# Query, key and value projections in three rounded passes, for two sequences at once

## The reference, cut to what matters

```python
# 1. retention: 16 heads of 16, over the 32 sequences
qkv = x @ W_qkv;  q, k, v = split(qkv)
ret = einsum('bhtd,bhsd->bhts', q, k) * decay          # causal decay mask
r = einsum('bhts,bhsd->bhtd', ret, v) + (q @ past_kv) * 256
x = layernorm(x + groupnorm(r))
# 2. causal attention of x over ctx (keys and values from ctx)
q = x @ Wq.T;  k = ctx @ Wk.T;  v = ctx @ Wv.T
x = layernorm(x + softmax(causal(q k^T / 4)) @ v @ Wo.T + bo)
# 3. two of 8 experts for each token, hidden size 1024
x = layernorm(x + sum over the top two of gate_e * (gelu(x @ w_fc[e] + b_fc[e]) @ w_proj[e] + b_proj[e]))
```

## Time and profile before

| | us |
|---|---|
| median of 3 runs | 1039.97 (1038.79 to 1041.47) |
| the profiled execution, its own time | 1039.19 |
| its span | 1037.0 |
| PE busy | 961.4 (93%) |
| DVE busy | 657.6 (63%) |
| ACT busy | 590.1 (57%) |

### The profile page before, as it was taken

The page is one execution under the profiler, slowest core; times in us unless marked ns, Lnnn a source line. Parts: engine busy times, 40 slices in busy tenths (PEclk is TensorE's granted clock), DMA queues, the critical chain, the costliest instruction groups (busy, mean ns, idle before and its releaser), DMA issues.

```text
span 1037.0 us, 30058 instructions
## 1 busy us (share of the span) xinstructions
PE 961.4 (93%) x10909; PEld 846.7 (82%) x10909; DVE 657.6 (63%) x2020; ACT 590.1 (57%) x1533; POOL 372.3 (36%) x630
## 2 busy tenths in 40 slices
PE   6799999999999999999988898999999999999950
PEld 4688888888888888888867897999999999999950
DVE  2456767667677677777764565665575765575537
ACT  3355555555555555555555564665575665575534
POOL 0224544445444444444453432322223222223223
PEclk9799999999999999999998999999999999999985
DMA  8101151111111111113011234442525342522327
GB/s 271 52 23 53 38 181 42 54 63 38 58 43 53 63 38 59 42 54 108 23 48 42 47 73 122 103 81 41 142 42 133 92 92 41 141 43 42 48 39 317
DMA packets 56931, 79.91 MB, mean 77 GB/s; under 512 B 5681, under 2 KB 45873, under 8 KB 56561
## 3 DMA queue, kind: packets, MB, share of 16 engines
q1 hardware_dynamic: 41072, 58.50, 17.3%
q0 software_dynamic: 13536, 18.16, 10.1%
q10 hardware_dynamic: 2208, 1.73, 0.6%
HBM read 52.10 MB, written 29.71 MB: 79 GB/s over the span
## 4 chain that ended last, share of the span: by engine, by line
PE 65%; DVE 16%; ACT 5%; issue 5%; POOL 4%; DMA 3%; SPq 1%; ACTq 0%; DVEq 0%; POOLq 0%
PE bank L724 15%; PE bank L738 10%; DVE row_max L1111 7%; PE bank L483 5%; PE bank L740 5%; PE bank L598 3%; PE bank L498 3%; PE bank L473 3%; PE bank L551 3%; PE bank L643 3%; PE bank L523 3%; PE bank L629 2%; ACT h_f L1017 2%; PE bank L518 2%; POOL grstd L1487 2%
## 5 line engine op out<-in xcount | busy, mean ns | idle before, releaser
L724 PE MATMUL bank<-xs_hi,w_both 128*128 128x256 f32 x1152 | 242.2, 287 | 0.1
L1011 ACT ACTIVATE h_hi<-bank,bfc_s 128x256 fp32r<-128x256 f32 x288 | 139.6, 485 | 163.0 <-PE bank L724 157.5
L1529 POOL DMA_INDIRECT residual_sum<-y_w,meta_i x72 | 116.6, 1619 | 308.1 <-DVE y_w L1356 284.2
L1314 DVE TENSOR_TENSOR h_lo<-h_f,h_hi 128x256 fp32r<-128x256 f32 x288 | 121.6, 425 | 150.6 <-ACT h_f L1017 146.5
L738 PE MATMUL bank<-w_both,h_hi 128*128 128x512 f32 x544 | 200.5, 398 | 1.3 <-DVE h_lo L1314 1.2
L724 PEld LDWEIGHTS bank<-xs_hi,w_both 128*128 128x128 f32 x1152 | 191.5, 190 | 8.4 <-issue 2.2
L724 PE MATMUL bank<-xs_lo,w_both 128*128 128x256 f32 x576 | 162.9, 283 | 0.0
L740 PE MATMUL bank<-w_both,h_lo 128*128 128x256 f32 x544 | 153.2, 282 | 0.0
L1017 ACT ACTIVATE h_f<-bank,bfc_s 128x256 f32<-128x256 f32 x288 | 138.9, 482 | 4.3 <-DVE h_lo L1314 3.6
L738 PEld LDWEIGHTS bank<-w_both,h_hi 128*128 128x128 f32 x544 | 102.8, 189 | 20.2 <-DVE h_lo L1314 3.7
L724 PEld LDWEIGHTS bank<-xs_lo,w_both 128*128 128x128 f32 x576 | 109.8, 191 | 0.1
(11 more groups left out here) (167 smaller groups left out, 1928.9 us busy)
## 6 DMA issues: line engine op xcount, KB each, us to landing
rows<-sent_rows SPq DMA_DIRECT2D x37, 258.0 KB
xcT<-in_turned SPq DMA_DIRECT2D x32, 256.0 KB, 2.7
w_raw<-in_w_fc SPq DMA_DIRECT2D x8, 1024.0 KB
w_raw<-in_w_proj SPq DMA_DIRECT2D x8, 1024.0 KB
x_t<-in_x SPq DMA_DIRECT2D x32, 128.0 KB, 2.6
residual_sum<-x_row SPq DMA_DIRECT2D x32, 128.0 KB, 1.7
last_in<-residual_sum SPq DMA_DIRECT2D x8, 512.0 KB, 7.3
result<-last_out SPq DMA_DIRECT2D x8, 512.0 KB, 2.6
```

Of the source, the lines that this page charges most:

```text
L724: last = mm(ps_h(g, j), w[:, at:at + P], v[:, k, :], start=(n == 0), stop=(n == 3 * NCH - 1))
L1011: A(h_hi[j % 4][:, :], ps_h(g, j), ACT.Gelu_apprx_tanh, bias=bias)
L1314: V.tensor_tensor(h_lo[j % 4][:, :], h_f[j % 2][:, :], h_hi[j % 4][:, :].bitcast(f32), ALU.subtract).then_inc(s["h_split"], 1)
L1529: G.indirect_dma_start(total, bass.IndirectOffsetOnAxis(meta_i[:, half:half + 1], 0), y_w[:, half, :], None, compute_op=ALU.add)\
```

## The change

The projections no longer use float32 matmuls. Each operand is split into a rounded part (`_hi`, made by an ACT copy) and the rest (`_lo`, a DVE subtraction), and three matmuls of rounded operands, hi by hi, hi by lo and lo by hi, take the place of one. The queries and keys are computed for two sequences at once (`pair_run`, m = 0 to 15), 256 columns in each matmul: `prep_k(m)` and `prep_q(m)` stand in the odd steps, `prep_kx(m)` in the even ones, `prep_v` in each step for the next sequence. Each of the four is 12 matmuls of 256 columns, recorded at L500. Activations are loaded for a pair at once (`load_turned`), split by `x_high` on ACT and `x_low` on DVE, one half in each step. In even steps `att_scores` moves ahead of `att_proj` and `qx`. The weights are split once before the first step (`w_high`, `w_low`). The output biases of experts 1 to 7 (`bproj_rest`) are loaded after the steps, into space that the attention has left. The stages that are kept stand in the order that they had on DVE, ACT and POOL; on ACT the copies of the projections follow their stages.

The core of the diff:

```diff
-        h_hi = [sb(f"h_hi{i}", [P, SLOT], f32r) for i in range(4)]
-        h_lo = [sb(f"h_lo{i}", [P, SLOT], f32r) for i in range(4)]
+        h_parts = sb("h_parts", [P, 8, SLOT], f32r)
+        h_hi = [h_parts[:, i, :] for i in range(4)]
+        h_lo = [h_parts[:, 4 + i, :] for i in range(4)]
+        xc_hi = [h_parts[:, 4 * i:4 * i + 4, :].rearrange("p (a k) n -> p a k n", a=2) for i in range(2)]
...
+        def over(name, shape):
+            with ExitStack() as raw:
+                loaded = raw.enter_context(nc.sbuf_tensor(name + "_raw", shape, f32))
+            return loaded, ab(name + "_lo", shape, f32r)
+        wqk_raw, wqk_lo = over("wqk", [P, NCH, 2 * C])
...
+        xc_raw, xc_lo = zip(*(over(f"xc{i}", [P, 2, NCH, 2 * T]) for i in range(2)))
+        qkT = ab("qkT", [P, 2, NCH, 2 * T])
+        q_own = ab("q_own", [P, NCH, PAIR, 2 * T])
+        kxT = [ab(f"kxT{i}", [P, NCH, 2 * T]) for i in range(2)]
...
+            def load_turned(m, a):
+                if m >= 2:
+                    sp.wait_ge(s["prep_v"], 2 * m - 2)
+                    apart(sp)
+                sp.dma_start(xc_raw[m % 2][:, a, :, :].rearrange("p k t -> p (k t)"),
+                             turned[m, :, a * 2 * C:(a + 1) * 2 * C]).then_inc(s_turned[m % 2][a], 16)
...
+            load_turned(0, 0)
+            sp.dma_start(wqk_raw[:, :, :], w_qkv[:, 0:2 * C].rearrange("(k p) n -> p k n", p=P))\
+                .then_inc(s["got_wqk"], 16)
+            load_turned(0, 1)
...
+                if k >= 0 and k % 2:
+                    for a in range(2):
+                        pair_run(load_turned, (k + 3) // 2, a)
...
+            sp.dma_start(bproj_rest[:, :, :].rearrange("p e c -> p (e c)"),
+                         b_proj[1:E, :].rearrange("e c -> (e c)").partition_broadcast(P)).then_inc(s["got_bias"], 16)
...
-            def prep_qk(c):
-                pe.wait_ge(s["kx_out"], c.n + 1)
+            def three(to, passes):
+                last = None
+                for n, (left, right) in enumerate(passes):
+                    last = mm(to, left, right, start=(n == 0), stop=(n == len(passes) - 1))
+                return last
+            def channels(m, a, w_hi, w_lo, first_col):
+                x_hi, x_lo = xc_hi[m % 2], xc_lo[m % 2]
+                for j in range(NCH):
+                    at = slice(first_col + j * P, first_col + (j + 1) * P)
+                    last = three(ps_prep[:, j * 2 * T:(j + 1) * 2 * T],
+                                 [(w[:, k, at], v[:, a, k, :]) for k in range(NCH)
+                                  for w, v in ((w_hi, x_hi), (w_hi, x_lo), (w_lo, x_hi))])
+                return last
+            def prep_k(m):
+                if m:
+                    pe.wait_ge(s["v_out"], 2 * m)
+                else:
+                    pe.wait_ge(s["w_split"], 1)
+                pe.wait_ge(s["xc_split"], 2 * m + 1)
+                channels(m, 0, wqk_hi, wqk_lo, C).then_inc(s["prep_k"], 1)
+            def prep_q(m):
+                pe.wait_ge(s["k_out"], m + 1)
+                if m == 0:
+                    pe.wait_ge(s["w_split"], 2)
+                channels(m, 0, wqk_hi, wqk_lo, 0).then_inc(s["prep_q"], 1)
+            def prep_kx(m):
+                pe.wait_ge(s["v_out"], 2 * m + 1)
+                if m == 0:
+                    pe.wait_ge(s["w_split"], 4)
+                channels(m, 1, wk_hi, wk_lo, 0).then_inc(s["prep_kx"], 1)
+            def prep_v(c):
+                m, h = c.n // 2, c.n % 2
+                if h:
+                    pe.wait_ge(s["kx_out"], m + 1)
+                else:
+                    pe.wait_ge(s["q_out"], m + 1)
+                    pe.wait_ge(s["xc_split"], 2 * m + 2)
                 if first(c, 1):
-                    pe.wait_ge(s["got_wqk"], 16)
-                for m in range(2 * NCH):
-                    for k in range(NCH):
-                        last = mm(ps_prep[:, m * P:(m + 1) * P], wqk_s[:, k, m * P:(m + 1) * P],
-                                  xcT[c.r][:, 0, k, :], start=(k == 0), stop=(k == NCH - 1))
-                last.then_inc(s["prep_qk"], 1)
-            def prep_kx(c):
-                pe.wait_ge(s_turned[c.r], 16 * (c.g + 1))
-                if not first(c, 1):
-                    pe.wait_ge(s["v_out"], c.n)
-                if first(c, 1):
-                    pe.wait_ge(s["got_wk"], 16)
-                for m in range(NCH):
-                    for k in range(NCH):
-                        last = mm(ps_prep[:, m * P:(m + 1) * P], wk_s[:, k, m * P:(m + 1) * P],
-                                  xcT[c.r][:, 1, k, :], start=(k == 0), stop=(k == NCH - 1))
-                last.then_inc(s["prep_kx"], 1)
-            def prep_v(c):
-                pe.wait_ge(s["qk_out"], c.n + 1)
-                if first(c, 1):
-                    pe.wait_ge(s["got_wv"], 32)
-                for i, w in enumerate((wvr_s, wva_s)):
-                    for k in range(NCH):
-                        last = mm(ps_prep[:, i * C:(i + 1) * C], xcT[c.r][:, i, k, :], w[:, k, :],
-                                  start=(k == 0), stop=(k == NCH - 1))
+                    pe.wait_ge(s["w_split"], 3)
+                at = slice(h * T, (h + 1) * T)
+                x_hi, x_lo = xc_hi[m % 2], xc_lo[m % 2]
+                for a in range(2):
+                    last = three(ps_prep[:, a * C:(a + 1) * C],
+                                 [(v[:, a, k, at], w[:, a, k, :]) for k in range(NCH)
+                                  for v, w in ((x_hi, wv_hi), (x_hi, wv_lo), (x_lo, wv_hi))])
                 last.then_inc(s["prep_v"], 1)
...
             def step(k):
+                odd = k % 2
                 run(ret_scores, At(k))
                 run(att_back, At(k - 3))
                 run(x1_turn, At(k - 1))
-                run(prep_v, At(k))
+                if odd:
+                    pair_run(prep_k, (k + 1) // 2)
+                else:
+                    run(att_scores, At(k - 2))
                 run(att_proj, At(k - 3))
                 run(qx, At(k - 1))
-                run(att_scores, At(k - 2))
+                if odd:
+                    run(att_scores, At(k - 2))
                 run(ret_values, At(k))
                 run(rank, At(k - 4))
-                run(prep_kx, At(k + 1))
+                if odd:
+                    pair_run(prep_q, (k + 1) // 2)
+                else:
+                    pair_run(prep_kx, k // 2)
                 run(x2_turn, At(k - 3))
                 run(gn_mean, At(k))
                 run(y_back, At(k))
                 run(max_scores, At(k - 1))
                 run(att_values, At(k - 2))
-                run(prep_qk, At(k + 1))
+                run(prep_v, At(k + 1))
                 run(logits, At(k - 3))
...
+            def x_high(m, a):
+                act.wait_ge(s_turned[m % 2][a], 16 * (m // 2 + 1))
+                A(xc_hi[m % 2][:, a, :, :], xc_raw[m % 2][:, a, :, :], ACT.Copy)\
+                    .then_inc(s["xc_high"], 1)
+            def k_out(m):
+                act.wait_ge(s["prep_k"], m + 1)
+                A(qkT[:, 1, :, :].rearrange("p k t -> p (k t)"), ps_prep[:, :], ACT.Copy).then_inc(s["k_out"], 1)
+            def q_out(m):
+                act.wait_ge(s["prep_q"], m + 1)
+                A(qkT[:, 0, :, :].rearrange("p k t -> p (k t)"), ps_prep[:, :], ACT.Copy)
                 for j in range(PAIR):
-                    last = A(q_own[:, :, j, :], ps_prep[:, 0:C].rearrange("p (k t) -> p k t", k=NCH), ACT.Copy,
+                    last = A(q_own[:, :, j, :], ps_prep[:, :].rearrange("p (k t) -> p k t", k=NCH), ACT.Copy,
                              scale=own_head[j])
-                last.then_inc(s["qk_out"], 1)
-            def kx_out(c):
-                act.wait_ge(s["prep_kx"], c.n + 1)
-                A(kxT[c.r][:, :, :].rearrange("p k t -> p (k t)"), ps_prep[:, 0:C], ACT.Copy)\
+                last.then_inc(s["q_out"], 1)
+            def kx_out(m):
+                act.wait_ge(s["prep_kx"], m + 1)
+                A(kxT[m % 2][:, :, :].rearrange("p k t -> p (k t)"), ps_prep[:, :], ACT.Copy)\
                     .then_inc(s["kx_out"], 1)
...
+                if k == -1:
+                    act.wait_ge(s["got_small"], 16)
+                    w_high(0)
+                    x_high(0, 0)
+                    w_high(1)
+                    x_high(0, 1)
+                    w_high(2)
                 run(att_back_out, At(k - 3))
                 run(x1_T_out, At(k - 1))
-                run(v_out, At(k))
+                if k >= 0:
+                    pair_run(x_high, (k + 2) // 2, odd)
+                if odd:
+                    pair_run(k_out, (k + 1) // 2)
                 run(qx_out, At(k - 1))
                 for r in range(2):
                     run(att_exp, At(k - 2), r)
                 run(y_out, At(k))
                 for r in range(2, NT):
                     run(att_exp, At(k - 2), r)
-                run(kx_out, At(k + 1))
                 if k == -1:
```

(27 more changed lines are left out.)

86 lines of the change are left out of this document (48 added, 38 removed).

## The result

| | before | after |
|---|---|---|
| median, us | 1040.01 (1038.79 to 1041.47) | 1074.99 (1073.15 to 1076.31) |
| ratio to before, 95% interval | | 1.0334 (1.0312 to 1.0357) |
| the profiled execution, its own time | 1039.19 | 1074.04 |
| its span | 1037.0 | 1072.0 |
| third `gn_moments` of the span | 53.86 | 55.41 |

The change makes the kernel 3.3% slower. The forecast was 1066, the range 1038 to 1087. All but 2 of the 35 us lie within the steps.

A forecast was written before the change was run, and what follows sets the result against it. A step was taken as 10.14 us set by PE and 6.03 by DVE and POOL. Terms 11.0 + 10.0 - 1.0 + 0.8 - 1.3 + 6.8 gave +26.3, on 1039.2 and 0.8 for the median 1066 us, range 1038 to 1087.

The forecast's parts named there:

- the hidden stretch: From `gn_mean` to the next `o_turn`: 6.03 us that DVE and POOL set, with PE's work in it hidden.
- The stall: Even steps: `att_scores` waits for `ret_decay` to free its banks and holds `att_proj` and `qx`; `gn_mean` 1.00 us later.
- I move all up to `ret_decay` by 0.26: After `o_turn`, with shorter ACT copies ahead: DVE's stages start 0.26 us earlier, `ret_decay` at 1.59 in place of 1.85.
- The delay of 1.62: From the end of `ret_decay` to the stage behind `att_scores`: 1.62 us, read from a step with weight splitting.
- The odd step: Odd steps, PE's stretch from `o_turn` to `gn_mean`: 10.04 us, 0.10 less than before.
- Behind a split: Steps where L1230 delays `ret_decay`: even ones 2.49 us more, odd ones 0.21 more.
- The clock: Even steps behind a split: PE idles over 2 us, the clock falls, 1.7 us lost in each of four, 6.8 together.
- in all even steps: Rival: the clock falls in every even step, since one bank of four works at a time; 18.7 more, 1085 us; chance 0.18.
- behind the even steps 22 to 28 only: Sign to show the forecast: a granted clock of 0.5 in the trace behind these four steps and nowhere else.
- The rival in which they run at the pace of float32: Projection passes at 0.22 us, not 0.12: three groups in PE's first stretch cost 1.2 more each, 1120 us; chance 0.03.
- `x_low` is hidden: DVE ahead of `gn_moments`: the 0.69 us instruction is covered by 0.15 in even steps, by more in odd ones.
- The faster rival: Even steps: banks come free before PE asks, no stall; `gn_mean` at 8.60, 1.54 less; 1014 us; chance 0.15.

The follow-up runs named there:

- e6: e1 with two more matmuls of 512 bf16 columns ahead of `prep_v`, in the hidden stretch: 1029.64 us, ratio 0.9884.
- e7: e1 with two matmuls of 512 columns ahead of `prep_q` and `prep_kx`, in the stretch that PE sets: 1042.55 us, ratio 1.0021.
- e3: The changed kernel with two of the three passes of `prep_v`, 8 matmuls in place of 12: 1091.01 us, ratio 1.0483.
- e4: The changed kernel with eight idle matmuls ahead of `att_scores` in the four even steps behind a weight split: 1068.79 us, ratio 1.0263.
- e1: The changed kernel with `att_scores` back behind `att_proj` and `qx` in even steps, all else kept: 1032.03 us, ratio 0.9924.
- e8: e1 with the projections in float32 matmuls of 256 columns again, pairs and order kept: 1044.38 us, ratio 1.0024.
- e9: e1 with DVE's part of the expert's weight split moved from ahead of `ret_decay` to the next step's wait for `gn_mean`: 1026.57 us, ratio 0.9863.

## Why the prediction was right

**The steps and the hidden stretch.** From `gn_mean` to the next `o_turn` it was 6.03, and it is 6.03 now: 326.59 to 332.62. e6, e7 and e3 show the same by cost.

**The stall.** The even step's `gn_mean` was forecast at 11.14 from `o_turn`; it came at 11.44, so the step grew by 1.30 and not by 1.00. The steps of the sum, with the times of after:

| from `o_turn` | forecast | measured |
|---|---|---|
| L1281 `rden` | 0.65 | 0.67 |
| `ret_decay` starts | 1.59 | 1.72 |
| `att_proj` starts | 5.69 | 5.83 |
| `rank` starts | 9.42 | 9.66 |
| `gn_mean` starts | 11.14 | 11.44 |

The step that failed is "I move all up to `ret_decay` by 0.26". `att_norm` did begin where I said, but `ret_decay` starts 1.16 after `ret_scores` (L562, 315.71), and that stage stands behind `o_turn` on PE as before. It is 1.16 in the odd step too (333.18 to 334.34) and was 1.29 before, so I read its first bank as what is late next; no run tests this. Half of the gain of 0.26 is gone by it. A tenth more went between `att_proj` and `rank`, where `att_proj` itself took 0.96 to the next stage in place of 0.86, and 0.06 in the twelve matmuls (1.50, L500 at 334.66 to L707 at 336.17, in place of 1.44). The delay of 1.62 between the last `ret_p` and the stage behind `att_scores`, from rows 6, held: 1.63. One number of the text was wrong and entered no sum: `prep_v`, `att_proj` and `qx` cost 3.58 before (2.27 to 5.85) and not 4.3; it was the last bank that came free at 4.33.

**The odd step.** Forecast 0.10 less, measured 0.08 more: 3.55 to `att_proj` (332.62 to 336.17) where I had 3.44, and the 0.06 of `prep_q`. Over ten steps that is 1.4 us apart from the forecast.

**Behind a split.** Forecast 2.49 more at the full clock, that is 19.1; e4 has 19.05 to 19.32. A step of after (k = 22) with its wait:

```profile
387.15 3.44 PE L662 MATMUL bank<-qx_own,kxT 32*128 32x256 f32 x15 [1.78 <-DVE ret_p L1223]
...
391.91 2.07 PE L707 MATMUL bank<-wo_s,attT 128*128 128x256 f32 x4
```

and after's windows of 3 us from there:

```profile
387.00:390.00 3.00, 2.85 (x17) 2.31 (x21) 1.89 (x4) 0.00 (x0) 1.70 (x2) 0.59 0.26 91
390.00:393.00 3.00, 3.00 (x29) 2.14 (x22) 0.00 (x0) 0.00 (x0) 0.00 (x0) 0.50 0.00 0
393.00:396.00 3.00, 3.00 (x47) 2.70 (x49) 1.62 (x8) 0.83 (x3) 0.50 (x1) 0.77 0.00 0
```

PE has almost nothing from 385.4 to 387.15, and the clock is then at 1.2 GHz until about 394. `att_proj` (L707) takes 1.86 to the next stage in place of 0.96.

**The clock.** Four falls of 1.7 were forecast, and e4 gives 1.7 on average. One more came in an ordinary even step (k = 16, 1.7 us). Step k = 8 is 0.4 longer at the full clock: `rank` waits 0.71 there for `hot_b` in place of 0.37, also in e3 and e4 (17.82), and why is open. The rival "in all even steps" was wrong, but its mechanism is not absent: e3 shows how near it is. What was held against it, that PE is never idle for more than 0.3 at a time, fails: in each step PE waits 0.70 for `row_max`, where it had no such wait before, since `prep_v` in the hidden stretch is shorter than `prep_qk` was. That hidden saving had been put at nothing; it costs nothing in length, but by e3 a longer wait there brings more falls of the clock. And a low clock "behind the even steps 22 to 28 only" was too narrow: it came in k = 16 and, at 0.73 (before: 0.89), in step 2.

**The sum.** All in us:

| term | forecast | measured |
|---|---|---|
| ordinary even steps | 11.0 (eleven) | 15.1 (ten; the eleventh is step 2) |
| even behind a split, clock included | 10.0 + 6.8 | 16.9 |
| ordinary odd steps | -1.0 | 0.4 |
| odd behind a split | 0.8 | 0.4 |
| last step | -1.3 | -1.3 |
| start, with step 2 | 0 | 1.5 |
| from the last `gn_moments` to the end | 0 | 2.0 |
| together | 26.3 | 35.0 |

The mechanism, its places and its order of size were right. The largest of the mis-sized terms is the ordinary even step, 1.3 in place of 1.0, with the one fall of the clock in it. The 1.5 of the start is no firm number, since the time ahead of the first `gn_moments` differs by up to 3.9 between executions of kernels that are the same there (after, e1, e4). The last 2.0 lie between the last step and the first experts. It isn't the load of `bproj_rest`, since e1 has the same load and takes 510.3 there, before 510.5 and after 512.5. The wait for routed rows is 1.3 of it (5.9 in after, 4.6 before); the rest is open.

**The passes.** Twelve at 1.50 against 1.44. The rival in which they run at the pace of float32 is refuted by this and by e8. An estimate by the ratio of four passes to three, from the Trainium skill (FP8 and Floating Point Precision, TensorE Precision Notes), would have made them 1.30; the trace of after has 1.50.

**`x_low` is hidden.** L1215 is done at 325.72, and `gn_moments` still waits 0.42 for `gn_mean`: hidden by more than the 0.15 I gave it. DVE was through `put` 11.34 from `o_turn`, as forecast (11.3), and `gn_mean` came later than forecast.

**The faster rival** asked for a delay under 1.54 in an even step, where I had 2.54. Measured against its own 8.60 the delay is 2.84 (`gn_mean` at 11.44), against e1's even step 2.12, over 1.54 either way. Even with the order put back, e1 stays above its 1014: the even step loses 0.82 and not 1.53, and the odd one nothing.

## What to carry to other kernels

Work that stands ahead of a wait is its cover. When a stage is made shorter or moved, ask which wait the old one covered; here `prep_v`, `att_proj` and `qx`, 3.6 us of PE, hid the time that DVE needs to read four banks, and moving the consumer of these banks to the front cost 2.1 us in each even step. Read the gain of a change of arithmetic apart from that of the new order: the three passes gave 12 us and the order took 43. And where one engine waits in each step for another (DVE for `gn_mean` here), a piece of work that stands ahead of the critical stage can be moved into that wait: e9 did so and gave 5.5 us.
